# Two FFN and attention layers on one core: late attention's running sum split into high and low parts, and a new instruction order for all engines

## The chip, the cores and the metric

The kernel runs on one core of a Trainium2 chip. The metric is the time of one execution in microseconds (us) on the device; the median of three runs is compared.

## The reference

The input has 8 sequences of 256 tokens with 128 channels, 2048 tokens in all. Six blocks follow one another, each with a residual:

```python
x = x + 0.5 * _L0_ffn_ref(_layernorm(x), ...)    # MOE0_A: 16 experts, top 2, gelu, 128 -> 256 -> 128
x = x + _L0_attn_ref(_layernorm(x), ...)         # ATT0: a global sum over each sequence
x = x + 0.5 * _L0_ffn_ref(_layernorm(x), ...)    # MOE0_B: the weights of MOE0_A
x = x + 0.5 * _L1_ffn_ref(_layernorm(x), ...)    # MOE1_A: 16 experts, top 2, relu, 128 -> 128
x = x + _L1_attn_ref(_layernorm(x), ...)         # ATT1
x = x + 0.5 * _L1_ffn_ref(_layernorm(x), ...)    # MOE1_B: the weights of MOE1_A
```

The attention that the change touches is ATT1, with 16 heads of 8 channels:

```python
kv = jnp.einsum('blhd,blhe->blhde', k, v)
kv_cumsum = jnp.cumsum(kv, axis=1)
k_cumsum = jnp.cumsum(k, axis=1)
out = jnp.einsum('blhd,blhde->blhe', q, kv_cumsum)
```

## The kernel before

The tokens are cut into 4 chunks of 512 (4 tiles of 128 tokens). Every block of every chunk is computed for all experts; the top-2 weights (`comb`) are zero for the experts not chosen.

**Main loop.** MOE0_A and MOE0_B make 8 pairs of block and chunk, times 16 experts: 128 slots. In one slot, PE forms the hidden layer in two halves of three float32r products each (`mm3`, L906 to L908, into the three buffers of `ph`), ACT applies gelu (L600, into `g`), DVE multiplies by the expert's weights (L866, `hw`, from `bc`, which DMAs broadcast from `comb_rows`), and two slots later PE adds the second product to `py` (L1133). In the turns, one slot is two steps `m`: step a issues the hidden layer, step b the second product.

**The rest** stands in three streams that share the engines with the main loop. `l` (light) holds layer norms (`ln`: POOL L388 forms 1/sqrt, DVE L682 `xn`, PE L963 transposes, ACT L496 and DVE L688 split the result into a high part `xbh` and a low part `xbl`), routing (`rt`, up to `comb`, DVE L728), transposes of `comb` (`ct`, PE L989, ACT L507) and the adding of a chunk's FFN to `X` (`c0`). `h` (heavy) holds the preparation of weights (`w1`, `wt`), ATT0 (`a0`: DVE L748 to L763, then PE L1012, a gelu on ACT L532, PE L1016, and `X` at DVE L767), ATT1 (`a1`) and the FFNs MOE1 (`f1`) of the first three chunks. `k` (late) holds MOE1_A, ATT1 and MOE1_B of the last chunk: `LATE = [("g1", MOE1_A, 3), ("b1", ATT1, 3), ("g1", MOE1_B, 3)]`. It works in buffers of the main loop (`ph`, `w2s`, `hw`, `g`, `bc`, `w1h`, `w1l`), and so starts when that has ended.

An FFN of MOE1 takes 4 groups of 4 experts for each tile: PE L1041 to L1043 into one of three buffers (`ps`, late `ph`), ACT L551 with one relu for each expert (into `stage`, late `bc`), POOL L448 adds halves, DVE L794 reduces into `red`, POOL L441 adds to `X`.

ATT1: projections (PE L1058 to L1060), relu and exp on ACT (L563, L564), `qk` on DVE (L804). For each tile, POOL forms the outer products `kvo` (L414, 1024 wide). A running sum over tokens is a product with the triangular matrix `tri`, and for the second tile of a sequence also one of the first tile with `ones`. It is written in two ways:

- **Exact** (chunks named in `EXACT_CUM`): PE multiplies `kvo` in float32, L1087.
- **Split** (the others): ACT copies `kvo` to float32r (`kvh`, L575), DVE subtracts that from `kvo` (`kvl`, L812), and PE adds two float32r products, L1090 and L1091.

Then DVE multiplies by q (L824) and reduces (L829); after the last tile come a division (L841), transposes (PE L1098), a copy (ACT L586), the output projection (PE L1103) and `X` (DVE L850).

**The order.** Each engine runs its instructions in the order in which they are written, and waits at semaphores. `drive` sets this order from the strings in `TURNS`: "h4 l3 m4" takes four steps of `h`, three of `l` and four of `m`. There is one string for each engine; SP, which issues DMAs, has its own fixed program. Each chain above, of one chunk, is so spread over five queues.

Of the kernel before, what the change touches and what calls it, by code (L numbers as in the profile page):

```python
# [3 lines left out]


TURNS = {
# [19 lines left out]
}  # L26

# [9 lines left out]
def build_program(nc, x, wq, bq, wk, bk, wv, bv, wo, bo, Wr, br, W1, b1, W2, b2,  # L37
# [4 lines left out]
    ACT = mybir.ActivationFunctionType  # L42
# [21 lines left out]
    MOE0_A, ATT0, MOE0_B, MOE1_A, ATT1, MOE1_B = range(6)  # L64
    PIECES = [(0, 4), (4, 4), (8, 4), (12, 4), (12, 2), (14, 2)]
    TILES = TOK // P
    EXACT_CUM = (3, 4, 5, )
    LAG = 2
    PE_GATES = 3
    QUARTERED = {(MOE1_A, 0): False, (MOE1_B, 0): False, (MOE1_A, 1): False, (MOE1_B, 1): False}  # L70
# [3 lines left out]
    with ExitStack() as ctx:  # L74
# [147 lines left out]
        def ntiles(c):  # L222
            return PIECES[c][1]
# [65 lines left out]
        def split_tiles(c):  # L289

            late = ("b1", ATT1, c) in LATE
            before = [t[2] for t in (LATE if late else HEAVY) if t[0] in ("a1", "b1")]
            return sum(ntiles(t) for t in before[:before.index(c)] if t not in EXACT_CUM)

# [73 lines left out]
        def _(pool):  # L368
# [33 lines left out]
            def a1_(l, c):  # L402
                late, signal, b, done, n, k = attn1(c)

                def outer(t):
# [3 lines left out]
                    if t >= TPS:  # L409
                        if c in EXACT_CUM:  # L410
                            pool.wait_ge(signal["cum_ps"], 2 * (done + t - t % TPS))
# [67 lines left out]
        def _(act):  # L479
# [76 lines left out]
            def a1_(l, c):  # L556
# [12 lines left out]
                def high(t):  # L569
                    if c in EXACT_CUM:  # L570
                        return
                    act.wait_ge(signal["kv"], done + t + 1)
                    if t >= TPS:
                        act.wait_ge(signal["cum_ps"], 2 * (done + t - t % TPS))
                    nc.scalar.activation(b["kvh"][:, t % TPS, :], b["kvo"][:, t % TPS, :], ACT.Copy).then_inc(signal["kvh"], 1)  # L575
# [35 lines left out]
        def _(dve):  # L611
# [185 lines left out]
            def a1_(l, c):  # L797
# [10 lines left out]
                def low(t):  # L808
                    if c in EXACT_CUM:
                        return  # L810
                    dve.wait_ge(signal["kvh"], split_tiles(c) + t + 1)
                    V.tensor_tensor(u["kvl"][:, t % TPS, :], u["kvo"][:, t % TPS, :], u["kvh"][:, t % TPS, :].bitcast(f32),  # L812
                                    ALU.subtract).then_inc(signal["kvl"], 1)
# [87 lines left out]
        def _(pe):  # L901
# [144 lines left out]
            def a1_(l, c):  # L1046
# [28 lines left out]
                for t in range(n):  # L1075
                    if c in EXACT_CUM:
                        pe.wait_ge(signal["kv"], done + t + 1)
# [3 lines left out]
                    for b in range(2):  # L1081
# [3 lines left out]
                        for i in range(first, t + 1):  # L1085
                            if c in EXACT_CUM:
                                ins = T.matmul(ps[:, b, :], (tri if i == t else ones)[:, :], u["kvo"][:, i % TPS, part], start=i == first, stop=i == t)  # L1087
# [92 lines left out]
```

## Time and profile before

| | us |
|---|---|
| median of 3 runs (693.88 to 695.51) | 694.1 |
| the profiled execution's own time | 697.73 |
| its span, first to last instruction | 695.8 |
| PE busy | 641.5 (92%) |
| DVE busy | 468.4 (67%) |
| ACT busy | 436.3 (63%) |
| POOL busy | 187.8 (27%) |

The span is what the profile's rows add up to; the execution's own time is 1.9 us longer. PE's mean granted clock is 0.969 of full speed. The shares are averages over stages that differ: a stretch in which PE is always busy, up to about 557 us, and the rest.

### The profile page before, as it was taken

How to read it: one execution, taken by the hardware profiler on the slowest of the kernel's cores; microseconds unless marked ns; L12 is line 12 of the kernel's file. 1: busy time of each engine (PE TensorE's matmuls, PEld its weight loads, DVE VectorE, ACT ScalarE, POOL GpSimd, SP SyncE). 2: the span in 40 equal slices, each digit the busy share in tenths (PEclk: the TensorE clock that was granted, in tenths of full speed). 3: DMA queues.
4: the chain of work that ended last, by engine and by line, in shares of the span. 5: the costliest groups of instructions: out<-in, count | busy, mean ns of one | idle time of the engine just before them, and what ended most of it. 6: DMA issues, size and time to landing. Idle time of an engine off the chain costs nothing.

```text
span 695.8 us, 7583 instructions
## 1 busy us (share of the span) xinstructions
PE 641.5 (92%) x2361; PEld 408.2 (59%) x2361; DVE 468.4 (67%) x1063; ACT 436.3 (63%) x928; POOL 187.8 (27%) x132
## 2 busy tenths in 40 slices
PE   4999998999999899999999999999999967879784
PEld 3556564556556465676566666565766645555562
DVE  6588457634347955647799858879875577389542
ACT  4454455644446654697775495785489535988495
POOL 3120010200011101044251044051016252576465
PEclk9899999999999999999999999999999988999898
DMA  8842622155324213402133312204231000000000
GB/s 249 203 82 63 107 75 54 31 101 87 97 60 61 60 38 105 103 27 63 34 61 63 80 42 54 68 1 106 56 57 27 0 1 0 0 16 2 15 15 17
DMA packets 26737, 41.44 MB, mean 60 GB/s; under 512 B 1784, under 2 KB 9032, under 8 KB 26696
## 3 DMA queue, kind: packets, MB, share of 16 engines
q1 hardware_dynamic: 25128, 37.80, 24.9%
q10 hardware_dynamic: 1568, 3.15, 1.5%
q8 instruction: 19, 0.31, 0.2%
q14 instruction: 22, 0.18, 0.1%
HBM read 39.64 MB, written 1.31 MB: 59 GB/s over the span
## 4 chain that ended last, share of the span: by engine, by line
PE 67%; ACT 14%; DVE 11%; issue 5%; POOL 2%; DMA 0%; SPq 0%; POOLq 0%; ACTq 0%; DVEq 0%
PE py L1133 27%; PE ph L906 7%; PE ph L908 7%; PE ph L907 7%; ACT stage L551 7%; ACT bc L551 4%; PE ps L1041 2%; PE ps L1043 2%; PE ps L1042 2%; PE ph L1087 2%; DVE stage L760 1%; PE ps L1090 1%; PE py L1136 1%; ACT g L600 1%; PE ps L1091 1%
## 5 line engine op out<-in xcount | busy, mean ns | idle before, releaser
L600 ACT ACTIVATE g<-ph,b1col 128x512 f32<-128x512 f32 x256 | 172.3, 694 | 133.5 <-PE ph L908 121.1
L1133 PE MATMUL py<-hw,w2s 128*128 128x512 f32 x512 | 244.6, 601 | 1.5 <-DVE hw L866 1.5
L866 DVE TENSOR_TENSOR hw<-g,bc 128x1024 f32<-128x1024 f32 x125 | 161.6, 1301 | 86.9 <-ACT g L600 81.7
L1133 PEld LDWEIGHTS py<-hw,w2s 128*128 128x128 f32 x512 | 96.0, 192 | 77.6 <-issue 62.8
L906 PE MATMUL ph<-xbh,w1h 128*128 128x512 f32 x256 | 136.6, 534 | 0.6 <-ACT g L600 0.6
L388 POOL TENSOR_TENSOR rstd<-vare,mhalf 128x4 f32<-128x4 f32 x24 | 36.3, 1514 | 359.3 <-DVE vare L676 359.2
L551 ACT ACTIVATE stage<-ps,comb 128x128 f32<-128x128 f32 x384 | 107.2, 569 | 12.9 <-PE ps L1043 9.6
L908 PE MATMUL ph<-xbh,w1l 128*128 128x512 f32 x256 | 102.9, 402 | 0.0
L907 PE MATMUL ph<-xbl,w1h 128*128 128x512 f32 x256 | 102.6, 401 | 0.0
L448 POOL TENSOR_TENSOR stage<-stage 128x1024 f32<-128x1024 f32 x24 | 57.3, 2389 | 67.3 <-ACT stage L551 67.3
L906 PEld LDWEIGHTS ph<-xbh,w1h 128*128 128x128 f32 x256 | 49.4, 193 | 31.1 <-issue 21.5
L907 PEld LDWEIGHTS ph<-xbl,w1h 128*128 128x128 f32 x256 | 49.5, 193 | 25.5 <-issue 18.7
L908 PEld LDWEIGHTS ph<-xbh,w1l 128*128 128x128 f32 x256 | 48.8, 191 | 11.4
L1041 PE MATMUL ps<-weh,xbh 128*128 128x512 f32 x96 | 47.5, 495 | 3.9 <-ACT stage L551 3.1
L682 DVE TENSOR_SCALAR xn<-X,mv,rstd 128x128 f32<-128x128 f32 (+1 forms) x96 | 32.6, 402 | 14.2 <-POOL rstd L388 14.1
L794 DVE TENSOR_REDUCE red<-stage 128x128 f32<-128x1024 f32 x24 | 29.1, 1214 | 19.1 <-POOL stage L448 18.8
L1042 PE MATMUL ps<-weh,xbl 128*128 128x512 f32 x96 | 39.1, 407 | 0.0
L1043 PE MATMUL ps<-wel,xbh 128*128 128x512 f32 x96 | 39.0, 406 | 0.0
L551 ACT ACTIVATE bc<-ph,comb 128x128 f32<-128x128 f32 x128 | 35.2, 569 | 5.2 <-DVE comb L728 3.3
L414 POOL TENSOR_TENSOR stage<-qk,v 128x1024 f32<-128x1024 f32 x12 | 25.2, 2109 | 26.4 <-DVE kvl L812 15.2
L1041 PEld LDWEIGHTS ps<-weh,xbh 128*128 128x128 f32 x96 | 18.9, 197 | 19.3 <-ACT stage L551 14.4
L600 ACT ACT_TABLE_LOAD x22 | 28.2, 1283 | 0.7 <-DVE hw L866 0.3
(200 smaller groups left out, 847.8 us busy)
## 6 DMA issues: line engine op xcount, KB each, us to landing
bc<-comb_rows SPq DMA_DIRECT2D x31, 1024.0 KB, 8.4
stage<-in_L_ffn_W_dram SPq DMA_DIRECT2D x4, 512.0 KB, 6.8
X<-in_L_attn_x_dram SPq DMA_DIRECT2D x4, 256.0 KB, 10.4
out_dram<-X SPq DMA_DIRECT2D x4, 256.0 KB, 2.3
comb_rows<-combT SPq DMA_DIRECT2D x8, 32.0 KB, 6.5
bc<-comb_rows SPq DMA_DIRECT2D x1, 256.0 KB, 3.7
side<-in_L_attn_wq_dram SPq DMA_DIRECT2D x1, 64.0 KB, 7.0
side<-in_L_attn_wk_dram SPq DMA_DIRECT2D x1, 64.0 KB, 8.3
```

Of the source, the lines that this page charges most:

```text
L388: nc.gpsimd.tensor_tensor(rstd[:, 0:n], vare[:, 0:n], mhalf[:, 0:n], ALU.pow).then_inc(light["rstd"], 1)
L448: nc.gpsimd.tensor_tensor(both, both, other, ALU.add).then_inc(signal["half"], 2)
L551: ins = nc.scalar.activation(r[:, j % 2, :].rearrange("p (a d e) -> p d a e", a=4, d=D)[:, :, e // 4, e % 4], banks[:, u % 3, i * D:(i + 1 ...
L600: nc.scalar.activation(g[:, s % 2, h, 0:w], ph[:, (HC * s + h) % RING_PH, 0:w], ACT.Gelu, bias=b1col[:, HC * e + h:HC * e + h + 1]).then_i ...
L866: V.tensor_tensor(hw[:, s % RING_HW, :, 0:w], g[:, s % 2, :, 0:w], gates.unsqueeze(1).to_broadcast([P, HC, w]), ALU.mult).then_inc(hw_read ...
L906: T.matmul(dst, wh, xh, start=True, stop=False)
L907: T.matmul(dst, wh, xl, start=False, stop=False)
L908: return T.matmul(dst, wl, xh, start=False, stop=stop)
L1041: T.matmul(b, xbh[:, tile_(c, j)], weh[:, w], start=True, stop=False)
L1042: T.matmul(b, xbl[:, tile_(c, j)], weh[:, w], start=False, stop=False)
L1043: T.matmul(b, xbh[:, tile_(c, j)], wel[:, w], start=False, stop=True).then_inc(signal["y_ps"], 1)
L1133: ins = T.matmul(py[:, 0:cols], w2s[:, w], hw[:, s2 % RING_HW, h, 0:cols], start=e2 == 0 and h == 0, stop=False)
```

## The change

ATT1 of the last chunk goes from the exact form to the split form, and all strings of `TURNS` except that of SP are replaced. The lines of the file move down by 8 (L575 is L583 after, and so on). The number of steps of each stream stays the same on each engine. Two pieces of the diff:

```diff
-    "POOL": ("h18 m260 l44 h12 l8 h16 l9 h5 l2 h7 l8 h16 l8 h9 l3 h6 l4 h10 k7 h k2 h2 l2 h4 l4 h k6 h3 k10 h5 l4 h8 k8"),
...
-    EXACT_CUM = (3, 4, 5, )
+    EXACT_CUM = ()
```

What `EXACT_CUM` does shows on PE in the last chunk's ATT1, tiles 3 and 4. Before (`w2s` is `kvo`; `ps<-weh` rows are MOE1_B of chunk 1 between them):

```order
L1087 MATMUL ph<-w2s,tri 128x512 x2
L1041 MATMUL ps<-weh,xbh 128x512
L1042 MATMUL ps<-weh,xbl 128x512
L1043 MATMUL ps<-wel,xbh 128x512
L1087 MATMUL ph<-w2s,ones 128x512
L1087 MATMUL ph<-w2s,tri 128x512
L1087 MATMUL ph<-w2s,ones 128x512
L1087 MATMUL ph<-w2s,tri 128x512
```

After, the last tile (`w1h` and `w1l` are `kvh` and `kvl` there):

```order
L1098 MATMUL ph<-w1h,ones_r 128x512
L1099 MATMUL ph<-w1l,ones_r 128x512
L1098 MATMUL ph<-w1h,tri_r 128x512
L1099 MATMUL ph<-w1l,tri_r 128x512
L1098 MATMUL ph<-w1h,ones_r 128x512
L1099 MATMUL ph<-w1l,ones_r 128x512
L1098 MATMUL ph<-w1h,tri_r 128x512
L1099 MATMUL ph<-w1l,tri_r 128x512
```

Each float32 product has become a pair; in all, 12 products become 24.

ACT, from the end of the main loop on. `ysb` is the copy that ends it; `kvh<-stage` are the four copies of chunk 2's ATT1; `exs` is the exp of the routing for MOE1_A of the last chunk, and `bc<-ph` its relus. Before:

```order
L606 ACTIVATE ysb<-py 128x512
L575 ACTIVATE kvh<-stage 128x1024 x2
L496 ACTIVATE xbh<-pl 128x512
L575 ACTIVATE kvh<-stage 128x1024 x2
L502 ACTIVATE exs<-shf 128x64
L551 ACTIVATE bc<-ph,comb 128x128 x32
```

After:

```order
L583 ACTIVATE kvh<-stage 128x1024
L614 ACTIVATE ysb<-py 128x512
L583 ACTIVATE kvh<-stage 128x1024
L504 ACTIVATE xbh<-pl 128x512
L510 ACTIVATE exs<-shf 128x64
L559 ACTIVATE bc<-ph,comb 128x128 x8
L583 ACTIVATE kvh<-stage 128x1024
L559 ACTIVATE bc<-ph,comb 128x128 x12
L583 ACTIVATE kvh<-stage 128x1024
```

The third and fourth copy have moved behind the routing's exp and the first relus; the first has moved ahead of `ysb`. On DVE, in the same place, a subtraction (L812), two of the attention's products (L824), a reduction and the steps of the divisor (L835 to L838) have moved from ahead of `comb` to behind it, and `xbl` follows `xn` at once.

POOL, where the last chunk's MOE1_A ends (`red_late` is its last tile) and its ATT1 starts with a layer norm (`rstd`). `stage<-stage` are the half sums of chunk 0's MOE1_B. Before:

```order
L448 TENSOR_TENSOR stage<-stage 128x1024
L441 TENSOR_TENSOR X<-X,red_late 128x128
L448 TENSOR_TENSOR stage<-stage 128x1024
L441 TENSOR_TENSOR X<-X,red 128x128
L388 TENSOR_TENSOR rstd<-vare,mhalf 128x4
L448 TENSOR_TENSOR stage<-stage 128x1024
```

After:

```order
L449 TENSOR_TENSOR X<-X,red_late 128x128 x2
L456 TENSOR_TENSOR stage<-stage 128x1024
L396 TENSOR_TENSOR rstd<-vare,mhalf 128x4
L456 TENSOR_TENSOR stage<-stage 128x1024
L449 TENSOR_TENSOR X<-X,red 128x128
L456 TENSOR_TENSOR stage<-stage 128x1024
```

The last addition to `X` now comes before the first half sum of the other FFN, and the layer norm's step comes one half sum earlier.

## Rows read from the trace of the kernel before

**Rows 1.** Busy time by stretch: PE, PEld, DVE, ACT, POOL, granted clock, DMA share.

```profile
486.00:557.00 71.00, 70.47 (x278) 46.35 (x278) 49.61 (x116) 47.48 (x107) 19.19 (x12) 1.00 0.19 36
557.00:628.00 71.00, 55.07 (x232) 39.41 (x231) 49.19 (x113) 48.59 (x159) 37.92 (x25) 0.88 0.02 4
628.00:696.00 68.00, 51.40 (x175) 32.51 (x174) 36.73 (x73) 48.42 (x180) 38.54 (x27) 0.88 0.04 13
```

**Rows 2.** What PE waited for from 58 to 557 us: total, times, longest.

```profile
PE ps L1012 <- DVE side L763: 3.9, 3, 1.9
PE pl L989 <- DVE comb L728: 1.7, 3, 0.7
PE ps L1058 <- DVE X L767: 1.6, 2, 0.8
PE py L1133 <- DVE hw L866: 1.1, 1, 1.1
PE ps L1016 <- ACT side L532: 0.8, 1, 0.8
```

**Rows 3.** What ACT waited for from 557 us to the end.

```profile
ACT xbh L496 <- PE pl L963: 6.9, 2, 6.3
ACT stage L551 <- PE ps L1043: 6.9, 5, 3.5
ACT g L586 <- PE ph L1098: 5.6, 1, 5.6
```

**Rows 4.** Timeline of SP's queue and of PE at the start, and PE at 231 us.

```profile
27.27 0.50 SPq L358 DMA_DIRECT2D stage<-in_L_attn_Wq_dram  x1
32.59 0.42 SPq L360 DMA_DIRECT2D stage<-in_L_ffn_expert_b_dram  x1
41.65 0.63 PE L963 MATMUL pl<-ident,xn 128*128 128x128 f32 x4 [0.86 <-DVE xn L682]
42.69 1.98 PE L1133 MATMUL py<-hw,w2s 128*128 128x512 f32 x4 [0.41 <-DVE hw L866]
230.93 1.13 PE L1012 MATMUL ps<-side,wos 128*128 128x512 f32 x2 [0.48 <-DVE side L763]
```

**Rows 5.** Timeline of DVE at slot 64, then two slots from the chain of waits.

```profile
264.33 2.36 DVE L866 TENSOR_TENSOR hw<-g,bc 128x1024 f32<-128x1024 f32 x2 [4.65 <-DMA bc<-comb_rows]
268.74 1.72 PE py L1133 x4
271.87 1.72 PE py L1133 x4
```

**Rows 6.** Timeline from the main loop's last product on, PE, DVE and ACT.

```profile
556.79 1.12 PE L1136 MATMUL py<-combT,b2s 16*128 16x512 f32 x2
564.74 2.21 DVE L682 TENSOR_SCALAR xn<-X,mv,rstd 128x127 f32<-128x127 f32 x4
569.85 0.68 DVE L688 TENSOR_TENSOR xbl<-pl,xbh 128x512 fp32r<-128x512 f32 x1
577.94 6.98 ACT L551 ACTIVATE bc<-ph,comb 128x128 f32<-128x128 f32 x24 [3.33 <-DVE comb L728]
```

**Rows 7.** Timeline from the last chunk's ATT1 on, all engines.

```profile
606.16 0.46 POOL L441 TENSOR_TENSOR X<-X,red_late 128x128 f32<-128x128 f32 x1
617.61 0.36 PE L1058 MATMUL ph<-qkv1h,xbh 128*128 128x256 f32 x1 [1.50 <-DVE xbl L688]
652.53 0.69 DVE L850 TENSOR_TENSOR X<-ph,X 128x512 f32<-128x512 f32 x1 [2.43 <-PE ph L1103]
653.87 5.84 ACT L551 ACTIVATE stage<-ps,comb 128x128 f32<-128x128 f32 x20 [3.50 <-PE ps L1043]
671.36 17.11 ACT L551 ACTIVATE bc<-ph,comb 128x128 f32<-128x128 f32 x64
```

**Rows 8.** One line's instructions: duration in ns, least, median, most.

```profile
L575 ACT ACTIVATE kvh<-stage x12: 1041/1057/1067, 349.5 to 572.6; 128x1024 fp32r<-128x1024 f32 x12
L812 DVE TENSOR_TENSOR kvl<-stage,kvh x12: 1212/1218/2365, 351.1 to 580.5; 128x1024 fp32r<-128x1024 f32 x12
```

43 rows, old and new, of the table TURNS are left out of this document.

## The prediction

> **What bounds the kernel now.** I read busy time by stretch first, since the page's shares average over unlike stages. From 486 to 557 us PE is busy for 70.5 of 71 us; in the last 139 us it is busy for 106.5, and no engine is full: ACT is the nearest, with 48.6 + 48.4 = 97.0 us [rows 1]. So there are two kernels in one. Up to 557 us only a wait of PE, or less work on PE, is worth anything. After it, the end of ACT's queue counts. It holds 320 relus, and the last 64 of them take 17.11 us, 0.27 us each [rows 7], so about 86 of its 97 us are relus that no edit touches. What can shrink in the tail is the 42 us in which ACT is idle.
>
> Next the waits. Up to 557 us PE's named waits sum to 9.1 us over ten places [rows 2], nearly all where ATT0 ends (L1012, L1016, L1058) and where `ct` follows the routing too closely (L989). In the tail the largest waits of ACT are 6.3 us for the transposes of the layer norm ahead of the late MOE1_A, 5.6 us for those at the end of the late ATT1, and 6.9 us for PE in relus [rows 3]. None is a matter of capacity: in each, a chain crosses five queues in which other work stands ahead of it. An order can move them.
>
> **The split form alone.** It removes 12 float32 products of 128x512. The main loop's second products have that size, and two of them take 1.72 us: 0.86 each, 10.3 us of PE. It adds 24 float32r products of the width of those of the hidden layer, of which six take 3.13 - 1.72 = 1.41 us: 0.235 each, 5.6 us [rows 5]. That is 4.7 us of PE in a stretch where PE has 32 us idle: worth nothing by itself. It adds 4 copies of 1.06 us on ACT (4.2 us) and 4 subtractions of 1.22 us on DVE (4.9 us) [rows 8], both on the attention's own chain: POOL's product, copy, subtraction, product with `tri`. Bounds on what it costs: 0 if copies fall into ACT's idle time during that attention and the sums run while DVE works on the tile before; at the other end, copy and subtraction of every tile in series, 4 x 2.28 = 9.1, less the 4.7 of PE, 4.4 us. I take about 1, near the lower end. DVE is busy for 36.7 of the last 68 us [rows 1], and the new order lets the copy of a tile run behind relus that are ready. In exchange POOL's third product need no longer wait for both sums of the first two tiles, only for a subtraction.
>
> **The order up to 557 us.** I count the steps between a wait and what it waits for. A slot is 3.13 us on PE, of which the second product takes 1.72 and the hidden layer 1.41 [rows 5].
> - ATT0 of chunk 1: PE's o-product (L1012), transposes (L1016) and the next second product stood in a row and waited 0.48, 0.8 and 1.1 us [rows 4, 2]; now ATT0's projections stand half a slot earlier, one and a half slots lie between o-product and transposes, and DVE does `hw` before the routing, not after. I count 2.0 saved.
> - `ct` stands a slot or more behind its old place after the routing wherever it waited: its 1.7 go [rows 2]. One of the three waits is the shortest and lies right behind those just counted, so I take 1.3.
> - The projections of ATT1 wait 0.8 twice for `X` of ATT0 [rows 2]; for chunk 1 a hidden layer now stands between them, for chunk 0 nothing. 0.8 saved.
> - The other two waits at L1012 (1.9, and 3.9 - 1.9 - 0.5 = 1.5) stay: between ATT0's projections and o-product chunk 0 has as many steps as before and chunk 3 one less, and the chain from one to the other takes over 11 us.
> - Start: the third chunk's layer norm and routing move from slots 5 and 6 to slots 6 to 12, so the waits of 0.86 and 0.41 at slot 5 [rows 4] go: 1.3. Against it, the last part of `w1l` is now made behind slot 2's `hw`, about 20 us later, and SP issues the six L1 weights after it. Those issues take 5.7 us [rows 4], and PE needs the data at slot 7; by my count it waits up to 1. Net 0.9, with either sign possible at 1 us.
>
> Sum 5.0. I take off 1.0 for waits that so many moved steps will create, and count **4.0**, between 0 and 6.
>
> **The order in the tail.** From PE's last product of the main loop, 557.9, to the first late relu it is now 20 us: that relu starts at 577.94, after `comb`, and `xbl` ended at 570.5 although `xn` started at 564.7 [rows 6]; copies on ACT and attention work on DVE stood between. Below I lay the steps of the new order end to end, each with the duration that it has in the same timeline, and each queue's turn kept. After, each step follows its predecessor: `xn` at 563.3 (1.1 us of work; 2.2 now), transposes to 565.2, `xbh` to 565.8, `xbl` to 566.6, PE's routing to 567.8, one subtraction on DVE to 567.8, then the routing's 2.4 + 1.2 us, `comb` at 571.5. The relus start 6.4 us earlier. The two copies that now stand behind the first relus delay nothing that ACT could do earlier. I lose 0.4 again at the end of ATT1 of chunk 2: the late MOE1_A ends about 6.0 us earlier.
>
> Then the late ATT1. Its layer norm started after `X` at 606.6, its projections at 617.6, `X` was done at 653.2 [rows 7]. New order on POOL: the last `X` ahead of a half sum (2.4 us), `rstd` one half sum earlier. From there I count, on the trace's clock: `X` of the late MOE1_A 597.5, `rstd` done 601, projections 607.4 to 610.4 (ACT takes 12 groups of relus first), `qk` 612.7, first copy 615.8, second 620.1 (POOL now does a half sum between the first two products: 2.4 us lost), first sum reduced at 624.4, second 631.7, third 638.5, fourth 642, `X` 646.3. That is 6.9 ahead of 653.2, though from projections to `X` it takes 39 us instead of 36: the split costs what I allowed, and a bit. From 653.87 to the last relu ACT never stops: 34.6 us [rows 7]. It resumes at 646.7, waits 0.5 for the last `comb`, and what follows its last relu is the same. Tail gain **6.5 us**, between 1 and 8.
>
> **Sum.** 4.0 + 6.5 = 10.5 of a span of 695.8: 685.3. The profiled execution took 697.73 in all, so 1.9 lie outside the span and the median of 694.1 is 3.6 below it; I take the difference over: 694.1 - 10.5 = **683.6**.
>
> **A rule against the change.** DVE's subtraction took 1212 to 1218 ns in nearly all of its 12 places, but 2365 once, and the four operations of `xn` took 2.21 us at 564.74 while POOL worked [rows 8, 6]. So an overlap with POOL can cost one subtraction 1.15 us. Four of them: at most 4.6 us on the late chain, sum 688.2; by the median row, nothing. I keep nothing in the sum and 4.6 in the range. The Trainium skill (SBUF — State Buffer, section "SBUF: two separate sides") says that DVE with two SBUF inputs and a reading GpSimd hold a port pair in turns, each for a whole instruction. The trace agrees in one of twelve, by its greatest value.
>
> **Rivals.**
> - *The late chain eats the tail's gain.* Copies queue behind groups of relus (1.1 us each) on ACT, subtractions behind reductions on DVE. At the upper end of the split's cost, 4.4 for the 1 allowed, plus an early start of relus that stalls on buffers: tail 2, sum 694.1 - 4 - 2 = 688. For it: ATT1's four tiles serialise on DVE, which I have busy for 6 to 7 us a tile. Against: DVE idles for 31 of the last 68 us. Chance 0.15.
> - *No difference.* Main loop: `comb` of MOE0_B's chunk 1 is sent one slot later. DVE waited 4.65 us for it already, and PE needs its `hw` at 268.7, against 265.5 now [rows 5]; 2.5 us later leaves 0.7. A slower landing, the late L1 weights and a DVE held at ATT0's start could take 4 to 5 us, and the tail gives 3: about 692.5. Chance 0.10.
> - *Slower.* ACT is the tail's bound and gets 4.2 us more. If its idle time does not fall, the end moves out by 4.2, and with no gain ahead: 698.3. It decides when ACT's idle time after the main loop falls by less than 4.2 us of 42. For it: copies that wait for POOL keep ready relus behind them, as at the second copy. Against: the chain to `comb`, step by step. Chance 0.10.
>
> **How the numbers follow.** Forecast (680 to 687.5) 0.65; the rivals 0.15, 0.10, 0.10. A run of this kernel tells 0.3%, 2.1 us, from no change: up to 692.0 is faster, 696.2 and more slower. Faster 0.65 + 0.15 = 0.80, same 0.10, slower 0.10. Both best bounds, 6 and 8, give 680.1. The range goes a little past that, from 679, to 691.5, which takes in the first rival and the port's 4.6.
>
> **What would show it.** `comb` of the late MOE1_A 14 us after the main loop's last product instead of 20; ACT's idle time in the tail about 31 instead of 42 (42 - 6.5 - 4.2); the late ATT1 39 us from projections to `X`; PE's waits up to the main loop's end about 5 us; no float32 running sums, and 24 more products on L1098 and L1099. I am wrong if a wait of PE over 2 us stands in the main loop (L1 weights, or `bc` at slot 64), or if relus in the tail wait behind copies.

## The result and the profile after

| | before | after |
|---|---|---|
| median of 20 runs each, us (lowest to highest) | 695.21 (693.76 to 699.93) | 693.15 (688.45 to 695.16) |
| ratio of the times | | 0.9957, 95% interval 0.9941 to 0.9973 |
| profiled execution: span, us | 695.8 | 693.2 |
| mean granted clock of PE | 0.969 | 0.963 |

The change makes the kernel 0.43% faster, 2 to 3 us, where 683.6 was forecast, 1.5% less, and 693.15 lies above the range. The sign was right, the size was not. The execution times of the new kernel go with the mean clock that PE, the engine of the matrix products, was granted: nine of 20 are 694.2 to 695.2 us with a mean granted clock of 0.963, six are 688.5 to 690.2 with 0.970 to 0.975, five lie between. The profiled execution is one of the nine (695.09 us), and the profiled one of the kernel before, 697.73, is 2.5 us above its median too. So profiles of single executions are good for distances inside a stretch, not for the last microseconds of the whole. One execution of end_fill, 1064 us at a mean clock of 0.559, is counted in none of the ratios below.

Busy time by stretch of the changed kernel, columns as in [rows 1]:

```profile
486.00:557.00 71.00, 70.67 (x277) 46.02 (x276) 45.17 (x115) 48.17 (x108) 19.35 (x13) 1.00 0.21 37
557.00:628.00 71.00, 56.25 (x238) 41.49 (x237) 54.38 (x120) 50.03 (x159) 37.71 (x25) 0.88 0.02 4
628.00:696.00 68.00, 44.32 (x170) 30.13 (x168) 35.24 (x69) 49.71 (x183) 37.06 (x26) 0.86 0.04 13
```

ACT is busy for 99.7 us after 557, 2.7 more than before, and is idle for about 36 of 136 us instead of 42 of 139. 31 were forecast.

What PE waited for from 58 to 557 us, as in [rows 2]:

```profile
PE ps L1020 <- DVE side L771: 4.1, 4, 1.9
PE ps L914 <- POOL X L449: 1.0, 1, 1.0
PE ps L1066 <- DVE X L775: 0.8, 1, 0.8
PE pl L971 <- DVE xn L690: 0.6, 1, 0.6
PE py L1141 <- DVE hw L874: 0.3, 1, 0.3
```

The waits for `comb` (1.7) and for ATT0's transposes (0.8) are gone, one of the two at ATT1's projections too; the o-product of ATT0 still waits 4.1 us, where 3.4 were forecast to stay, and 1.6 us of waits are new.

The start, by windows of 4 us. Before:

```profile
26.00:30.00 4.00, 4.00 (x9) 2.10 (x9) 3.74 (x4) 1.75 (x3) 1.75 (x2) 0.50 0.55 116
34.00:38.00 4.00, 4.00 (x14) 2.30 (x14) 3.60 (x26) 3.46 (x5) 0.00 (x0) 1.00 0.52 126
```

After:

```profile
22.00:26.00 4.00, 1.55 (x4) 0.37 (x2) 2.31 (x13) 0.00 (x0) 1.03 (x1) 0.80 0.19 64
26.00:30.00 4.00, 3.63 (x11) 2.63 (x11) 3.17 (x4) 1.28 (x2) 1.89 (x2) 0.50 0.73 165
34.00:38.00 4.00, 4.00 (x8) 2.33 (x7) 3.80 (x12) 1.72 (x2) 0.00 (x0) 0.50 0.00 0
```

And the timeline of the same place, after:

```profile
22.48 0.87 DVE L679 BATCH_NORM_STATS2 stats<-X 128x6 f32<-128x128 f32 x4 [4.43 <-DMA X<-in_L_attn_x_dram]
26.37 1.09 PE L971 MATMUL pl<-ident,xn 128*128 128x128 f32 x4 [2.82 <-DVE xn L690]
37.23 0.63 PE L914 MATMUL ph<-xbh,w1h 128*128 128x512 f32 x1
40.26 0.40 PE L915 MATMUL ph<-xbl,w1h 128*128 128x512 f32 x1
```

The third column from the end is the granted clock, 0.50 for 1.2 GHz. The second chunk's input lands at 22.48; its layer norm now stands on PE ahead of slot 2's hidden layer, and PE is idle for 2.82 us (0.70 before). PE is granted half speed from 24.4 to 38.0 us, a stretch of 13.65 us that begins within this wait; before, from 24.9 us on, it was 6.83. Such a stretch is called a low stretch below. A product of 512 columns takes 0.63 us in it and 0.40 behind it. At half speed the additional 6.8 us cost up to 3.4 us.

The tail, timeline of PE, DVE and ACT, lines that answer to [rows 6] and [rows 7]:

```profile
556.32 1.12 PE L1144 MATMUL py<-combT,b2s 16*128 16x512 f32 x2
562.88 1.11 DVE L690 TENSOR_SCALAR xn<-X,mv,rstd 128x127 f32<-128x127 f32 x4 [0.53 <-POOL rstd L396]
565.83 0.69 DVE L696 TENSOR_TENSOR xbl<-pl,xbh 128x512 fp32r<-128x512 f32 x1 [1.84 <-ACT xbh L504]
571.99 1.26 ACT L559 ACTIVATE bc<-ph,comb 128x128 f32<-128x128 f32 x4 [2.19 <-DVE comb L736]
607.90 0.36 PE L1066 MATMUL ph<-qkv1h,xbh 128*128 128x256 f32 x1 [0.30 <-DVE xbl L696]
616.10 2.27 DVE L820 TENSOR_TENSOR w1l<-w2s,w1h 128x1024 fp32r<-128x1024 f32 x1 [1.90 <-ACT w1h L583]
618.42 0.79 PE L1098 MATMUL ph<-w1h,tri_r 128*128 128x512 f32 x1 [3.38 <-DVE w1l L820]
623.70 0.69 DVE L832 TENSOR_TENSOR w2s<-w2s,ph 128x512 f32<-128x512 f32 x1
645.86 1.11 PE L1106 MATMUL ph<-ident,hw 128*128 128x128 f32 x4 [3.32 <-DVE hw L849]
649.77 0.69 DVE L858 TENSOR_TENSOR X<-ph,X 128x512 f32<-128x512 f32 x1 [1.98 <-PE ph L1111]
651.11 5.58 ACT L559 ACTIVATE stage<-ps,comb 128x128 f32<-128x128 f32 x20 [3.50 <-PE ps L1051]
```

The first relu comes 15.7 us after the start of the main loop's last two products (L1144), not 21.1, and the projections of the late ATT1 come 51.6 us after it, not 60.8. But from there to `X` it takes 42.6 us, not 35.6. Two windows inside this attention, after:

```profile
618.30:625.10 6.80, 6.68 (x20) 5.61 (x21) 5.50 (x23) 2.58 (x7) 4.61 (x4) 0.50 0.14 39
645.60:652.50 6.90, 5.96 (x20) 4.90 (x21) 4.20 (x16) 1.99 (x6) 1.41 (x3) 0.51 0.13 38
```

Both set in at the end of a wait of PE, of 3.38 and 3.32 us, and in both PE runs at 1.2 GHz on the attention's own chain. Over the whole tail the clock is no lower than before: from L1144 (L1136 before) to the end it is 0.88 in both kernels. What changed is where the low stretches fall.

### The profile page after: what moved, and what is told of

Read it like the earlier page. It is cut to its first block, busy times and chain, and to the rows that moved or that the text cites. A ratio compares the mean times of both kernels' runs of the same rounds, so it can differ in the third digit from the quotient of the medians.

```text
span 693.2 us, 7594 instructions
## 1 busy us (share of the span) xinstructions
PE 636.9 (92%) x2361; PEld 410.0 (59%) x2361; DVE 464.2 (67%) x1067; ACT 438.5 (63%) x932; POOL 183.4 (26%) x132
## 4 chain that ended last, share of the span: by engine, by line
PE 60%; ACT 16%; DVE 10%; issue 8%; POOL 5%; DMA 0%; SPq 0%; POOLq 0%; ACTq 0%; DVEq 0%
PE py L1141 25%; ACT stage L559 7%; PE ph L914 7%; PE ph L916 7%; PE ph L915 7%; ACT bc L559 3%; DVE stage L768 1%; PE ps L1049 1%; POOL stage L456 1%; PE ps L1051 1%; PE ps L1050 1%; POOL rstd L396 1%; PE pl L971 1%; ACT g L608 1%; PE pl L988 1%
## 5 line engine op out<-in xcount | busy, mean ns | idle before, releaser
L874 DVE TENSOR_TENSOR hw<-g,bc 128x1024 f32<-128x1024 f32 x125 | 155.9, 1256 | 63.3 <-ACT g L608 47.0
L396 POOL TENSOR_TENSOR rstd<-vare,mhalf 128x4 f32<-128x4 f32 x24 | 31.7, 1322 | 359.1 <-DVE vare L684 358.9
L559 ACT ACTIVATE stage<-ps,comb 128x128 f32<-128x128 f32 x384 | 110.2, 568 | 13.8 <-PE ps L1051 13.6
L690 DVE TENSOR_SCALAR xn<-X,mv,rstd 128x128 f32<-128x128 f32 (+1 forms) x96 | 29.1, 367 | 18.8 <-POOL rstd L396 18.7
L559 ACT ACTIVATE bc<-ph,comb 128x128 f32<-128x128 f32 x128 | 36.6, 668 | 4.1 <-DVE comb L736 2.6
L1050 PE MATMUL ps<-weh,xbl 128*128 128x512 f32 x96 | 38.8, 404 | 0.0
L504 ACT ACTIVATE xbh<-pl 128x512 fp32r<-128x512 f32 x24 | 14.8, 618 | 29.2 <-PE pl L971 29.2
L422 POOL TENSOR_TENSOR stage<-qk,v 128x1024 f32<-128x1024 f32 x12 | 28.0, 2348 | 19.6 <-DVE qk L812 11.1
```

What stands on the lines that cost most here:

```text
L396: nc.gpsimd.tensor_tensor(rstd[:, 0:n], vare[:, 0:n], mhalf[:, 0:n], ALU.pow).then_inc(light["rstd"], 1)
L559: ins = nc.scalar.activation(r[:, j % 2, :].rearrange("p (a d e) -> p d a e", a=4, d=D)[:, :, e // 4, e % 4], banks[:, u % 3, i * D:(i + 1 ...
L874: V.tensor_tensor(hw[:, s % RING_HW, :, 0:w], g[:, s % 2, :, 0:w], gates.unsqueeze(1).to_broadcast([P, HC, w]), ALU.mult).then_inc(hw_read ...
L1050: T.matmul(b, xbl[:, tile_(c, j)], weh[:, w], start=False, stop=False)
```

## The experiments

The ratios compare with the kernel before on the same chip; the medians come from several chips, on which that kernel's own is 694.7 to 695.3. Because a median mixes executions with different clocks at the start, the table has distances from one profiled execution of each kernel beside it. "slot 20" is the end of slot 20's second gelu, counted from the span's start; "main" from there to the start of L1144; "relu", "proj" from that start to the first relu of the late MOE1_A and to the late ATT1's projections; "ATT1" from these to the end of its `X`; all in us, from the timelines. Where "main" is about 1.5 us under its neighbours (455.2 for 456.7), a low stretch of 3.41 us at 115 us was missing in that execution.

| kernel | median | ratio (95%) | slot 20 | main | relu | proj | ATT1 |
|---|---|---|---|---|---|---|---|
| before | 695.2 | | 97.0 | 459.8 | 21.1 | 60.8 | 35.6 |
| after | 693.15 | 0.9957 (0.9941 to 0.9973) | 99.6 | 456.7 | 15.7 | 51.6 | 42.6 |
| order_only | 694.1 | 0.9975 (0.9954 to 0.9997) | 98.6 | 456.6 | 15.7 | 51.6 | 43.1 |
| split_only | 706.6 | 1.0158 (1.0130 to 1.0187) | 100.1 | 459.8 | 21.1 | 59.4 | 46.8 |
| tail_new | 696.8 | 1.0011 (0.9991 to 1.0030) | 96.3 | 459.8 | 17.0 | 53.6 | 42.3 |
| start_old | 691.05 | 0.9942 (0.9918 to 0.9965) | 95.3 | 455.1 | 15.7 | 51.7 | 42.6 |
| start_2a | 692.4 | 0.9950 (0.9930 to 0.9970) | 98.4 | 456.7 | 15.7 | 51.6 | 42.6 |
| start_fill | 691.1 | 0.9931 (0.9906 to 0.9956) | 95.5 | 457.1 | 15.7 | 51.6 | 42.5 |
| sum_first | 693.4 | 0.9970 (0.9943 to 0.9997) | 97.6 | 455.3 | 15.7 | 51.7 | 42.6 |
| sum_pair | 696.0 | 1.0001 (0.9978 to 1.0025) | 95.2 | 455.3 | 15.7 | 51.6 | 46.9 |
| late_old | 690.3 | 0.9915 (0.9886 to 0.9944) | 98.2 | 455.7 | 15.7 | 55.7 | 39.1 |
| best | 689.6 | 0.9908 (0.9877 to 0.9939) | 95.5 | 455.3 | 15.7 | 55.9 | 36.1 |
| late_fill | 688.6 | 0.9916 (0.9886 to 0.9945) | 95.6 | 455.2 | 15.7 | 51.6 | 39.7 |
| best_fill | 686.2 | 0.9869 (0.9844 to 0.9894) | 95.2 | 456.7 | 15.7 | 55.7 | 38.2 |
| end_fill | 689.4 | 0.9901 (0.9867 to 0.9936) | 95.5 | 455.2 | 14.4 | 51.0 | 42.3 |
| all_fill | 686.6 | 0.9870 (0.9833 to 0.9906) | 95.6 | 455.1 | 14.4 | 51.0 | 40.6 |
| before_fill | 693.1 | 0.9971 (0.9943 to 0.9998) | 95.5 | 458.4 | 21.1 | 59.3 | 35.3 |

### The two halves of the change apart

**order_only**

```diff
-    EXACT_CUM = ()
+    EXACT_CUM = (3, 4, 5, )
```

> The changed kernel with its new order, but the late ATT1's running sums as before, 12 float32 products instead of the split (the empty steps stay where the copies and subtractions stood). In the profile of the changed kernel the late ATT1 took 42.6 us from its projections to X, where it took 35.6 before and 39 were forecast. Theory S (the split itself is what costs): without it, the late ATT1 falls to 35 to 37 us and the kernel is 4 to 6 us faster than the changed one, about 688. Theory O (the new order of POOL, PE and DVE inside that attention costs, the split about 1 as forecast): the late ATT1 still takes 40 us or more, and the time stays within 2 us of 693.

**split_only**

```diff
-    TURNS of after
+    TURNS of before; in b1 of the last chunk ACT's steps 1 to 13 spread over f1 of chunk 1, DVE's step 1 behind the layer norm
```

> The order of before with the split of the late ATT1: since a split needs its copies and subtractions spread over the products, seven empty or copy steps of ACT are moved behind relus and one of DVE behind the layer norm's subtraction; all else stands as before. Theory S: late ATT1 of 39 to 43 us instead of 35.6, and 3 to 6 us slower than before, 698 to 701. Theory O: at most 1 to 2 us slower, 695 to 697. Forecast term on record for the split alone: 1 us, between 0 and 4.4.

Without the split the late ATT1 takes 43.1 us, with it 42.6: theory S falls, it is not the split that made it long. In the exact form it has waits of its own, as POOL and DVE of order_only show:

```profile
626.41 1.96 POOL L423 TENSOR_TENSOR w2s<-w2s,hw 128x1024 f32<-128x1024 f32 x1 [7.61 <-PE ph L1096]
630.84 1.22 DVE L803 TENSOR_REDUCE red<-stage 128x128 f32<-128x1024 f32 x1 [4.07 <-POOL stage L457]
```

In the exact form POOL's third product must wait for PE's sums, and in the new order a half sum, and behind it DVE, wait for POOL. With the split POOL issues that product at 620.96, 13.1 us after the projections instead of 19.7. In the order of before the split costs 11.2 us (46.8 for 35.6), and the median of 706.6 lies above both expectations (698 to 701, 695 to 697). There I chose the places of the copies, and a low stretch of 17.07 us fell into that attention, so the figure is no price of the split in a fitting order. What the two runs show is that the order alone brings most of what the change brings (ratios 0.9975 and 0.9957, with intervals that overlap), and that the split at the places I chose does harm in the old order.

**tail_new**

```diff
-    TURNS of after
+    TURNS of before up to slot 129 of the main loop, what is left in the order of after
```

> The order of before up to slot 129 of the main loop (on POOL up to the layer norm of the late MOE1_A), from there the new order, with the split. The profiles give 2.3 us for the new tail (137.9 us from the main loop's end before, 135.8 after, and the sum of two steps), so 693. If the forecast's tail term of 6.5 were only hidden by chance in one execution: 689. If the part of the order up to the main loop's end is what made the changed kernel faster: 695, no change.

The main loop takes 459.8 us from slot 20 on, as before, and 456.7 with the new order: 3.1 us belong to the order up to 557. The tail is 0.1 us shorter than before (138.9 from L1144 to the end of the span, 139.0), while the new order gains 2.2 behind its own main loop; the median, 696.8, is no change. Steps that the new order has ahead of the cut come later here; that this is the cause was not tried.

### The start

**start_old** (PE, ACT and DVE up to slot 15 in the order of before), **start_2a** (one step of PE) and **start_fill** (useless products):

```diff
 start_2a, TURNS["PE"]
-h l h l m2 h l h l m2 h l m l m4 l2 m4
+h l h l m2 h l h l m2 h m l2 m4 l2 m4
 start_fill, in ln of PE
+                if (l, c) == (MOE0_A, 1):
+                    for _ in range(8):
+                        T.matmul(py[:, P:CH], w1h[:, 0:P], xbh[:, P:CH], start=True, stop=True)
```

> The changed kernel with the order of before on PE, ACT and DVE up to slot 15. Theory C (clock at the start): in the changed kernel's profile PE ran at 1.2 GHz for 13.65 us from 24.4 us on, before for 6.83, after a wait of 2.8 us at 26.37 for the second chunk's layer norm, which waited for its DMA; 6.83 us more at half speed cost 3.4 us. With the old start the low stretch is 7 us, slot 20 is reached 2.6 us earlier, and the median falls to about 690. Rival: the start is worth nothing in the median, since other low stretches come in its place: 693.

> The changed kernel with one step moved on PE: slot 2's first hidden half now stands ahead of the layer norm of the second chunk, as it did before the change, and not behind it. So PE has 1.3 to 2.5 us of products to do while it now waits 2.8 to 3.4 us for that chunk's DMA. Theory C (the idle stretch at 23.5 to 26.4 us sets off the long stretch at 1.2 GHz): the low stretch falls from 13.65 us to 3.4 or 6.8 and the median falls by 2 to 3.5 us, to 690 to 691. Rival W (only the wait itself counts): at most the wait, 1.3 us, 692. Rival N: nothing, the low stretch comes whatever stands there.

> The changed kernel with 8 useless products of 128x384 on PE ahead of the wait for the second chunk's layer norm (they write a part of a bank that nothing reads, the result is the same): about 2.6 us of products where PE was idle 2.8 us. They do no work that the kernel needs. Theory C: the low stretch gets shorter or goes, the median falls by 1.5 to 3.5 us though work was added. Rival W (the wait's place in the order counts, not the clock): no change, or up to 1 us slower, 693 to 694.

PE in start_fill, then its window from 26 us:

```profile
23.43 2.51 PE L971 MATMUL py<-xbh,w1h 128*128 128x384 f32 x8
27.40 0.40 PE L917 MATMUL ph<-xbl,w1h 128*128 128x512 f32 x1
```

```profile
26.00:30.00 4.00, 3.94 (x21) 3.22 (x21) 2.96 (x4) 2.50 (x4) 1.92 (x2) 0.83 0.88 172
```

The useless work fills the wait, the low stretch is 3.41 us long instead of 13.65, products take 0.40 us from 27.4 on, not from 38, and slot 20 is reached 4.1 us earlier than in the changed kernel. One profile alone does not prove this, since three other kernels with the changed kernel's start reached slot 20 early too (last section); in their profiles PE, slower up to there, did not wait for this DMA at all. But of start_fill's ten timed executions one has a mean clock below 0.970, of the changed kernel's twenty eleven have, and the work added did not lengthen it. That speaks for theory C and against rival W (only the place of the wait counts); the intervals of the two kernels overlap, so it is not settled. start_old gives 4.3 us, and none of its eight executions is at 0.963. start_2a gives 1.2 only:

```profile
26.37 0.77 PE L972 MATMUL pl<-ident,xn 128*128 128x128 f32 x4 [2.95 <-DVE xn L691]
```

There products ran at full speed from 17.7 us on, PE was done with slot 2's first half and still waited for the same DMA, and a low stretch of 10.24 us followed, where theory C wanted 3.4 or 6.8. So the moved step is not shown to be the cause of the wait. The order of before has that wait too, of 0.70 us in its profile and of 1.06 to 2.48 in those of start_old, tail_new, best, best_fill, all_fill and before_fill, with low stretches of 3.41 or 6.83 us, and in split_only a wait of 2.65 us for a gelu at 19.94 stood ahead of one of 13.65. The length of a low stretch does not simply follow that of the wait: behind 2.48 us in tail_new it was 6.83, behind 1.78 in sum_first 10.24. The medians, 691 for start_old and start_fill, agree in direction; their intervals overlap that of the changed kernel.

### The late ATT1

**sum_first** and **sum_pair**:

```diff
 sum_first, TURNS["DVE"]
-h2 m l h l k2 h2 k h k h2
+h2 m l h k2 h2 k l h k h2
 sum_pair, on top, TURNS["POOL"]
-h3 l h k l h k2 h2 k2
+h3 l h k2 l h k h2 k2
```

> The changed kernel with three steps moved on DVE, in the late ATT1: the first tile's product with its running sums and the second tile's subtraction come ahead of the last but one routing, which goes behind the second product (in the changed kernel they waited until 623.7 for sums that PE had done at 619.6). Theory O (the order of DVE inside the late ATT1 costs the 3.6 us above the forecast): the first product starts 3 to 4 us earlier, the late ATT1 falls from 42.6 to 39 to 41 us, the median by 1.5 to 3.5 us. Rival D (DVE is full there, 19.3 of 20.5 us, so what goes first only pushes the rest back): 42 us, no change.

> As the run with the first product moved ahead on DVE, and on POOL the second tile's product comes right behind the first, ahead of a half sum of 2.35 us (as before the change). Theory P (that half sum between the two products costs 2.4 us of the late ATT1, as the forecast's working said): 2 us off the late ATT1 on top. Rival D (DVE is the limit): nothing on top.

The first product of DVE with the sums came 3.7 us earlier after the projections, and the attention still took 42.6 us; sum_pair was 4.3 us worse. Theories O and P, as put there, are refuted; rival D (DVE is full) fits the first. The subtractions (least, median, most in ns), of sum_first:

```profile
L821 DVE TENSOR_TENSOR w1l<-w2s,w1h x4: 1214/1743/2692, 612.7 to 634.0; 128x1024 fp32r<-128x1024 f32 x4
```

And of sum_pair:

```profile
L821 DVE TENSOR_TENSOR w1l<-w2s,w1h x4: 1217/2269/3008, 610.3 to 635.2; 128x1024 fp32r<-128x1024 f32 x4
```

Moved so that they fall on POOL's work, they stretch from 1.2 to up to 3.0 us: 7.4 and 8.8 us for four, where four undisturbed ones take 4.9 and those of the changed kernel took 5.9. The longest, in sum_pair, beside what POOL did at that time:

```profile
616.21 3.01 DVE L821 TENSOR_TENSOR w1l<-w2s,w1h 128x1024 fp32r<-128x1024 f32 x1
616.18 1.95 POOL L423 TENSOR_TENSOR w2s<-w2s,hw 128x1024 f32<-128x1024 f32 x1
```

It is the cost beside POOL from [rows 8], 1.79 us here, larger than the 1.15 us for one that I had in the range.

**late_old** (after up to the end of the late MOE1_A, then the order of before, exact sums) and **best** (the start of start_old as well):

> The new order up to the last step of the late MOE1_A on each engine, from there the order of before, and the late ATT1's running sums in float32 as before. Only the late ATT1 and what follows it changes against the changed kernel. Theory O (it is the new order of the late ATT1, with 14 more relus, half sums and reductions inside it, that makes it long: 42.6 us with the split and 43.1 without it): from the late MOE1_A's last relu the projections take the 17.0 us of before instead of 13.7, the attention 35.6, what follows the same: 3.7 us off the changed kernel's tail, so about 690. Rival B (a fixed amount of relus stands ahead of the end, so an attention that is shorter only starts later, and ACT's idle time stays 28.5 us between the main loop's end and the attention's end): no change, 693.

> Both mends together: the order of before up to slot 15 on PE, ACT and DVE (691.1 by itself), the new order in the main loop and the late MOE1_A, the order of before with float32 sums from there on. By theories C and O the gains add: 691.1 - 3.7 = 687.4. If the late ATT1's order is worth nothing: 691.

Busy time from the projections to `X`, the third figure from the end being the granted clock, of late_old:

```profile
609.50:648.70 39.20, 35.71 (x135) 25.41 (x136) 28.25 (x61) 21.42 (x70) 21.90 (x16) 0.85 0.05 14
```

And of best:

```profile
606.70:642.80 36.10, 32.64 (x135) 22.70 (x136) 28.16 (x60) 21.39 (x70) 21.85 (x16) 0.93 0.05 15
```

The order is the same, and so is the work; with a clock of 0.85 it takes 39.2 us, with 0.93 36.1. So 3 us of the attention's length go with when PE is granted half speed. The tail from L1144 to the end is 136.7 and 134.1 us, after's 136.8. So late_old, whose median of 690.3 is what theory O expected, does not bear it out: its attention is 3.5 us shorter and begins 4.1 us later, and the tail is as long as after's. That is what rival B said, and the lower median lies elsewhere; best's tail is shorter at the higher clock.

**late_fill** and **best_fill** (9 products, at the second place):

```diff
+                    if late and t == 0:
+                        for _ in range(11):
+                            T.matmul(ps[:, 0, :], tri_r[:, :], weh[:, 0:CH], start=True, stop=True)
...
+                if late:
+                    for _ in range(11):
+                        T.matmul(ps[:, 2, :], tri_r[:, :], weh[:, 0:CH], start=True, stop=True)
                 pe.wait_ge(signal["att"], k)
```

> The changed kernel with useless products on PE in the late ATT1: 11 of 128x512 (2.6 us at full clock) ahead of the wait for the first tile's subtraction (3.38 us idle in the changed kernel, after which PE ran at 1.2 GHz from 618.3 to 625.1) and 11 ahead of the last transposes (3.32 us idle, then 1.2 GHz from 645.6 to 652.5). The result is the same. Theory C2 (of the 7 us that the late ATT1 takes more than before, 2 to 3 come from these stretches at half speed, as the two executions of the order of before, 39.1 us with a low stretch of 10.2 us and 36.1 with one of 3.4, suggest): 42.6 falls to 40 to 41, the median by 1 to 3 us. Rival D (DVE and the waits for POOL set its length, PE's speed is hidden): 42 to 43, the median unchanged, or up to 1 us slower for the products in the way.

> The kernel with both mends, and 9 useless products of 128x512 ahead of the last transposes of the late ATT1, where PE is idle for 2.8 us before 8 products and transposes on the path. If C2 holds there: 0.5 to 1.5 us faster than 689.6. If not: the same within 0.7 us.

The late ATT1 in windows, the changed kernel:

```profile
607.90:650.50 42.60, 32.64 (x141) 25.38 (x142) 34.65 (x66) 28.34 (x88) 26.25 (x18) 0.86 0.05 13
```

And late_fill:

```profile
602.40:642.10 39.70, 34.22 (x164) 25.38 (x165) 34.15 (x65) 28.20 (x88) 26.38 (x18) 1.00 0.04 13
```

And PE in late_fill where the two low stretches were:

```profile
612.99 0.50 PE L1103 MATMUL ph<-w1h,tri_r 128*128 128x512 f32 x1 [0.86 <-DVE w1l L822]
638.85 0.66 PE L1114 MATMUL ph<-ident,hw 128*128 128x128 f32 x4 [0.82 <-DVE hw L851]
```

With 22 products more the clock stays at 1.00, the transposes take 0.66 us instead of 1.11, and the attention 39.7 us instead of 42.6. C2 holds, D does not. The tail is 133.2 us instead of 136.8; the rest of the 4.5 us between the medians is not explained by these products. In best_fill a low stretch of 10.24 us began 1.2 us before its projections, ahead of the useless products, and its attention took 38.2 us. Its median, 686.2, is the lowest of all, 3.4 us under best's where 0.5 to 1.5 were expected; its profiled execution, the slowest of six, does not show where they come from.

### The main loop's end, the sum, and the kernel before

Useless products ahead of the transposes of the late MOE1_A's layer norm (12 in **end_fill**; in **all_fill** with those of late_fill and the start of start_old; 10, with 9 in the late ATT1, in **before_fill**):

```diff
+                if (l, c) == (MOE1_A, 3):
+                    pe.wait_ge(g_ready, HC * SLOTS)
+                    for _ in range(12):
+                        T.matmul(ph[:, 0, :], tri_r[:, :], weh[:, 0:CH], start=True, stop=True)
```

> The changed kernel with 12 useless products of 128x512 on PE (2.8 us) ahead of the transposes of the late MOE1_A's layer norm, where PE is idle for 3.31 us before it runs at 1.2 GHz for 10.24 us, with 10 products on the path to comb and the first relus. Theory C3: the low stretch shortens or goes, the first relu comes 14 to 15 us after the last product's start instead of 15.7, the median falls by 1 to 2.5 us (half of what PE does on the path between 563.7 and 574). Rival: PE is not what the path waits for there (DVE's routing and ACT are), 0 to 0.5 us.

> The new order and the split, with the order of before up to slot 15 and useless products at three places (ahead of the late MOE1_A's layer norm, ahead of the first sums of the late ATT1, ahead of its last transposes). If the gains add: 693.2 - 2.1 (start) - 4.5 (late ATT1's two places, which in its timed run held some luck at the start, 3 by its profile) - 1 = 685.6 to 687. The forecast on record for the change without any loss to the clock: 683.6.

> The kernel before, with useless products at the same places where it is idle: 10 ahead of the late MOE1_A's layer norm (idle 2.2 us) and 9 ahead of the last transposes of the late ATT1 (idle 2.8 us). In its profile the low stretches of the tail are 6.83, 6.83, 3.41, 6.83 and 3.41 us. If they cost what they cost in the changed kernel: 1 to 3 us less than before, 692 to 694. If not: 695.

From L1144 to the first relu, in end_fill:

```profile
550.60:565.00 14.40, 11.63 (x55) 8.79 (x55) 10.50 (x41) 3.45 (x5) 7.19 (x5) 0.89 0.01 2
```

14.4 us instead of 15.7, clock 0.89 instead of 0.74. By the projections 0.6 us of this is left, and the tail is 0.7 us shorter. The median fell by 3.8 us; 3 of them the tail does not explain, in the profile they lie at the start (slot 20 at 95.5). all_fill gives 686.6, as expected from adding; before_fill 693.1, within its 692 to 694, though its first relu comes no earlier (21.1). The tail of all_fill:

```profile
550.76:684.32 133.56, 104.67 (x441) 73.76 (x440) 89.27 (x188) 100.60 (x341) 75.93 (x52) 0.92 0.03 9
```

And of before_fill:

```profile
553.93:689.97 136.04, 107.58 (x426) 73.33 (x425) 86.03 (x185) 95.88 (x337) 76.54 (x52) 0.92 0.03 9
```

At the same clock, 0.92, the tails differ by 2.5 us, hardly more than the 2.2 of the untreated pair at 0.88. The medians of the two differ by 6.5 us and the profiled spans by 5.6, of which 3.3 lie in the main loop and none at the start, where PE, ACT and DVE have the order of before in both. So with the start's loss taken away and the clock eased in both, the change is worth about 6 us, not the 10.5 that I counted.

## Why the prediction was wrong, step by step

- **Order up to 557 us, 2.0 + 1.3 + 0.8 - 1.0 = 3.1 us: right.** From slot 20 to the last product 459.80 became 456.72 us, 3.1 less, and tail_new, which has the old order there, is back at 459.8. The named waits tell the same: all of PE's from 58 to 557 us fell from 10.0 to 7.1 us. Its terms were less exact than their sum: ATT0's chain saved 1.4 (I had 2.0), `ct` 1.7 (1.3), the projections 0.8, new waits took 1.6 (1.0), and small waits that I had not counted gave 0.6.
- **Start, 0.9 us gained: the step that failed first.** Slot 20 was reached 2.6 us later in the profiled execution. I compared PE's waits and not its clock. The waits of 0.86 and 0.41 us went, but one of 2.82 us stands at 26.37, for the second chunk's DMA, where PE waited 0.70 before; PE meets that layer norm half a slot earlier, a step that is not in my list, though start_2a, which takes it back, waited 2.95. All named waits of PE up to there are 1.2 us longer than before instead of 1.3 shorter. The other 1.4 us go with the clock, 13.65 us at 1.2 GHz instead of 6.83, which can take up to 3.4. That the start is worth 2 us in the median too is what start_old and start_fill suggest (691.1 for 693.15); why one execution has the long low stretch and another not stays open. The late `w1l` and L1 weights, at which I had looked, show no wait.
- **Chain to the first relus, 6.4 us earlier, 14 us after the last product: nearly right.** From the end of the last product 14.6, and 5.5 us earlier than before. The missing us is mostly clock (end_fill: 14.4 from its start, 15.7 without). The projections came 9.2 us earlier, where I had 10.2.
- **Late ATT1, 39 us: the step that failed second.** 42.6. With the clock at 1.00 it is 39.7, so the sum of durations was right within 0.7 us and wrong in taking PE's durations at full speed on either side of waits of 3.3 us. The first tile's sums are reduced 19.5 us after the projections where I had 17.0, the fourth tile's 37.1 where I had 34.6, and the transposes and the output projection behind them take another 1.2 more. The first tile's delay is not the cause by itself: in sum_first its product came 3.7 us earlier and the attention stayed at 42.6.
- **The split alone, 1 us, 0 to 4.4.** Not settled as a single number: in the new order it gains 0.5 us (42.6 for 43.1), in the old order, with places of my own, it costs 11.2. As a bound on any order, 4.4 was too low; it took subtractions at 1.22 us and a clock like that of before.
- **A rule against the change.** One of the four subtractions took 2.27 us, on the chain, 1.05 more: about the 1.15 for one that I priced, far from 4.6. The divisor's step L845 took 1.2 us where three others take 0.2, but it had taken 1.45 in the same place before.
- **Tail gain 6.5: measured 2.2** (139.0 became 136.8). Of the missing 4.3, 2.9 are the low stretches in the late ATT1 and 1.0 the later projections; 0.4 stay open. This counts against the durations of the profile before. It does not say that the clock took the gain from the new order alone: with useless products in both kernels the tails differ by 2.5.
- **The rivals.** "The late chain eats the tail's gain" had the right place and left 2 us, as measured, but its cause, copies behind relus, is not what the runs point to. "No difference" named a loss of 4 to 5 us at the start, also by other causes. "Slower" did not come: ACT's idle time fell by more than 4.2.
- **The base.** 694.1 was the median of three runs, 695.2 that of twenty.

The Trainium skill (TensorE: Matmul & The Clock Gate, section "HAM oscillation — how this bites in real kernels") reckons the loss as half of the time spent at half speed. The trace agrees where PE bounds: without the stretch of 3.41 us at 115 us, whose half is 1.7, the way from slot 20 to the last product is 1.5 us shorter. In the late ATT1 11.7 us at half speed (all of the first stretch, 4.9 us of the second) gave 2.9, about a quarter; that PE is on the path for only part of them is my explanation.

## What to carry to other kernels

Lay the granted clock beside the waits before you count a new order: around two waits of 3.3 us on PE the slow products took 2.9 us more, and that where PE is no bound, since the chain runs through it. Where a wait can't be moved, cheap products in it are a quick test of this, and here a mend (late_fill, 688.6 us). Give the kernel before the same mend before you put a price on the change: here it took 2 us off that kernel too. And compare several executions of each kernel at the start, where a dependence on DMA is met later or earlier from one to the next.

## What was not expected of the hardware

- Work that serves nothing made the kernel faster: 22 products of 128x512 in the late ATT1, 2.9 us off it. With 8 at the start slot 20 came 4.1 us earlier than in the changed kernel's profile, which other executions of that order reached without them.
- The same instructions take different times at the start. Up to slot 20 the kernels after, order_only, sum_first, sum_pair, late_fill, end_fill and late_old have one and the same order; they reached it at 99.6, 98.6, 97.6, 95.2, 95.6, 95.5 and 98.2 us. In the first three a low stretch of 13.65, 13.65 and 10.24 us is recorded there, in the last four none; but their products too took 0.63 us up to 33 us, in late_old up to 35.7. Why one execution gets one and another the other was not settled. In the late ATT1 of the new order the two low stretches came at nearly the same places in the profiles of seven kernels (after, tail_new, start_old, start_2a, start_fill, sum_first, end_fill), 10.2 to 11.5 and 37.5 to 38.8 us behind the projections; in the order of before they did not (10.24 us of it in late_old, 3.41 in best, for the same order).
- The record of the granted clock does not hold everywhere: from the first product on it says 1.00, but products of 512 columns follow one another at 0.43 us until 21.5 us in the kernel before, and at 0.23 after.
- An operation of DVE with two SBUF inputs took up to 3.01 us beside POOL, 1.22 alone.
